# One piece of a maxima spread ahead of a bank copy in ScalarE's program

## The reference

```python
xn = layernorm(layernorm(x)) * ln_gamma + ln_beta
q, k, v = split(xn @ w_qkv)                   # 16 heads of 64; q and k are rotated (rope)
scores = einsum('bhid,bhjd->bhij', rotate(q), rotate(k)) * 64 ** -0.5
probs = softmax(scores)                       # over the 1024 keys j
x = x + (einsum('bhij,bhjd->bhid', probs, v) @ w_out + b_out)
x = x + fp4_linear(silu(gate) * up, w_down)   # gate, up = fp4_linear(layernorm(x), w_gate / w_up)
```

## Time and profile before

| what | before |
|---|---|
| median of 3 runs | 1604.24 us (1603.17 to 1604.52) |
| profiled execution | 1607.2 us, span of its instructions 1605.4 us |
| PE busy | 1512.1 us, 94% of the span |
| POOL busy | 1353.0 us, 84% |
| DVE busy | 1166.2 us, 73% |
| ACT busy | 890.3 us, 55% |
| max_rows pieces (L655) | 256 of 375 ns mean, 64 spreads |
| max_copy (L666) | 186 of 597 ns mean |

### The profile page before, as it was taken

The page is one execution under the profiler, slowest core; times in us unless marked ns, Lnnn a source line. Parts: engine busy times, 40 slices in busy tenths (PEclk is TensorE's granted clock), DMA queues, the critical chain, the costliest instruction groups (busy, mean ns, idle before and its releaser), DMA issues.

```text
span 1605.4 us, 25645 instructions
## 1 busy us (share of the span) xinstructions
PE 1512.1 (94%) x9257; PEld 789.6 (49%) x9257; DVE 1166.2 (73%) x1562; ACT 890.3 (55%) x1383; POOL 1353.0 (84%) x793
## 2 busy tenths in 40 slices
PE   3799999999999999999999999999999999998677
PEld 1345555445545554545545554555545455554455
DVE  4777777677777777776777777777777777763787
ACT  1265565655555665656555666655655665663222
POOL 4589999788889889898888988998888899976774
PEclk9699999999999999999999999999999999999798
DMA  4111111111111111111111111111111111100001
GB/s 131 45 28 47 48 43 44 47 47 43 28 47 47 34 47 47 40 48 47 42 35 40 48 34 47 48 39 47 47 44 45 29 47 36 41 17 23 7 14 33
DMA packets 69197, 67.10 MB, mean 42 GB/s; under 512 B 26512, under 2 KB 52432, under 8 KB 69072
## 3 DMA queue, kind: packets, MB, share of 16 engines
q1 hardware_dynamic: 69072, 65.46, 16.2%
HBM read 29.25 MB, written 2.62 MB: 20 GB/s over the span
## 4 chain that ended last, share of the span: by engine, by line
PE 82%; DVE 8%; ACT 5%; issue 4%; POOL 0%; DMA 0%; ACTq 0%; DVEq 0%
PE po L1130 29%; PE st L1117 18%; PE mx L1172 9%; PE ms L1153 8%; PE ms L1141 4%; PE ms L1198 4%; ACT max_rows L655 4%; PE ms L1189 4%; PE mx L1257 1%; PE ms L1180 1%; PE st L1257 1%; DVE negmax L871 1%; DVE probs L826 1%; DVE st L820 1%; DVE probs L1022 0%
## 5 line engine op out<-in xcount | busy, mean ns | idle before, releaser
L385 POOL TENSOR_TENSOR psum_keys<-psum_keys,probs 128x1024 f32<-128x1024 f32 x256 | 609.5, 2381 | 109.9 <-ACT probs L640 90.9
L640 ACT ACTIVATE probs<-st 128x1024 f32<-128x1024 f32 x512 | 498.5, 1030 | 131.0 <-PE st L1117 126.5
L1130 PE MATMUL po<-probs,v 128*64 128x512 f32 x2048 | 495.9, 605 | 0.0
L871 DVE TENSOR_REDUCE negmax<-mx 128x2 f32<-128x1024 f32 x318 | 388.3, 1221 | 125.8 <-PE mx L1172 125.6
L873 DVE TENSOR_REDUCE negmax<-mx 128x1 f32<-128x512 f32 x186 | 128.6, 691 | 215.8 <-PE mx L1172 215.8
L1130 PEld LDWEIGHTS po<-probs,v 128*64 128x64 f32 x2048 | 124.2, 136 | 256.2 <-issue 158.4
L1172 PE MATMUL mx<-keys_hi,queries_hi 64*128 64x512 f32 x1008 | 227.9, 448 | 9.2 <-ACT max_copy L666 5.4
L666 ACT ACTIVATE max_copy<-mx 128x512 f32<-128x512 f32 x186 | 111.1, 597 | 171.5 <-PE mx L1172 166.9
L1117 PE MATMUL st<-queries_hi,keys_lo 64*128 64x512 f32 x1024 | 204.0, 394 | 0.0
L1117 PE MATMUL st<-queries_lo,keys_hi 64*128 64x512 f32 x1024 | 202.1, 390 | 0.0
L1117 PE MATMUL st<-queries_hi,keys_hi 64*128 64x512 f32 x1024 | 201.8, 390 | 0.0
(11 more groups left out here) (161 smaller groups left out, 1803.5 us busy)
## 6 DMA issues: line engine op xcount, KB each, us to landing
kq<-sin_part SPq DMA_DIRECT2D x256, 128.0 KB, 2.4
rsum<-recips SPq DMA_DIRECT2D x128, 128.0 KB, 2.9
wqkv<-in_L_attn_w_qkv_dram SPq DMA_DIRECT2D x32, 192.0 KB, 2.8
resid<-in_L_attn_x_dram SPq DMA_DIRECT2D x4, 512.0 KB, 8.1
wout<-in_L_attn_w_out_dram SPq DMA_DIRECT2D x32, 64.0 KB, 2.6
out_dram<-resid SPq DMA_DIRECT2D x8, 256.0 KB, 2.3
sums<-sums_kept SPq DMA_DIRECT2D x64, 4.0 KB
spread<-sums SPq DMA_DIRECT2D x64, 4.0 KB, 1.6
```

What stands on the lines that cost most here:

```text
L385: nc.gpsimd.tensor_tensor(psum_keys[:, c], first, probs[:, (STEPS * P + i) % RING], ALU.add)\
L640: nc.scalar.activation(probs[:, step_n % RING], st[step_n % 2][:, :], ACT.Exp, scale=SCALE)\
L871: nc.vector.tensor_reduce(out, banks[:, :], AX.X, ALU.max, negate=True).then_inc(mx_free, 1)
L1130: last = mm(po[HD * a:HD * a + HD, :], v[:, P % 2, KEY_ORDER[jt], HD * a:HD * a + HD], probs[:, step_n % RING, a], start=(jt == 0), stop=( ...
```

## The change

In `spread_maxima` the call of `copy_ahead(P, d + 1)` moves from ahead of the spread to behind its first piece. The waits of the spread (for the transposition, for earlier scores, for the mask) are with that ahead of the copy, and the copy with its own waits is ahead of the other three pieces. No instruction is added or removed.

```diff
-        def spread_maxima(N, c):
+        def spread_maxima(N, c, P, d):
             filled(act, ("B", N, c))
             if N > 0 or c > 0:
                 act.wait_ge(st_ps, STEPS * (N - 1) + (JT if c == 0 else STEPS) + 2)
             act.wait_ge(mask_done, 1)
             for t in range(HALF):
                 last = nc.scalar.activation(max_rows[:, bass.ts(t, PART)], ms[:, 0:PART], ACT.Copy, scale=mask[:, t:t + 1])
+                if t == 0:
+                    copy_ahead(P, d + 1)
             last.then_inc(ms_free, 1)
...
                     if kind == "B":
-                        copy_ahead(P, d + 1)
-                        spread_maxima(X, u)
+                        spread_maxima(X, u, P, d)
```

## The result

The changed kernel takes 1590.84 us (median of 6 runs, 1590.47 to 1591.81), the kernel before 1604.59 in the same comparison (6 runs, 1603.17 to 1605.53): 13.75 us less, a ratio of 0.9914 with a 95% interval of 0.9903 to 0.9924. The forecast was 14.4 us less, and 1589.8 us. The profiled execution after has a span of 1588.7 us (1605.4 before) and a time of 1590.47 us. Three executions far out of line, two of the kernel before (1893.51 and 3633.75 us) and one of a variant (8068.79 us), are left out of all ratios.

The account below looks back on a forecast made before the run. TensorE bounds the kernel, held up by ScalarE's spread at 60 projections; 7.5 + 6.9 = 14.4 us won, other costs taken as 0, so 1604.24 us becomes 1589.8 us, range 1587 to 1598.

Parts of the forecast that it names:

- The ceiling of 0.25 and 0.23 us at 60 places: Projections behind a spread: at most 0.25 us at 30 places (L1153), 0.23 at 30 (L1198), 14.4 us in all.
- The 4% of max_rows in the chain: ScalarE's max_rows in the chain of waits: some 64 us of the span, said not to be what can be won.
- The piece lies in ScalarE's idle time and the copy is not late: ScalarE between transposition and copy: idle 2.64 us, copy has 0.25 us in hand; cost taken as 0.
- The rival that would have ended slower: ScalarE's queue: piece waits for the product, copy follows 0.39 us later; 8.4 us slower, 1612.6 us; chance 0.05.
- The release just meets TensorE's own earliest start: Bank ms free at 834.33, projection at 834.38, its undisturbed start; nothing to spare for L1153, 0.02 us for L1198.
- VectorE is next, and costs nothing: VectorE at the L1153 projections can follow by only 0.07 us for sure; its late mx release taken as 0 us.
- The 6.0 us that were kept for a late load: Weight load held for VectorE's mx release: if the matmul were as late, 0.20 us x 30 would go back.
- max_rows was to be gone from TensorE's waits: Sign of being right: max_rows gone from TensorE's waits and from the chain.
- TensorE's busy time was to stay the same: Sign of being right: TensorE's busy time unchanged while the span gets 14 us shorter.
- The six copy stalls shift with the rest: Six TensorE waits for the copied bank, 5.4 us in all: taken to cost 0 us, at most 1.5 us.

Follow-up runs that it names:

- Two and three pieces ahead: Two or three of the spread's four pieces ahead of the copy instead of one: 1590.41 us (ratio to before 0.9892) and 1590.88 us (0.9914).
- the extra piece behind: The change plus a useless fifth piece, written to an idle buffer, behind the copy: 1607.28 us, ratio to before 0.9999.
- d = 2 alone: One piece ahead of the copy only at d = 2, with d = 6 as in the kernel before: 1596.84 us, ratio to before 0.9951.
- the useless piece ahead: The change plus a useless fifth piece, written to an idle buffer, ahead of the copy: 1591.51 us, ratio to before 0.9901.
- the run with one memset: The change plus one tiny useless VectorE memset ahead of the rounding constants of y at three places: 1590.6 us, ratio to before 0.991.
- the four-ahead kernel: All four pieces of the spread ahead of the copy instead of one: 1607.02 us, ratio to before 1.0.

## Why the prediction was right, point by point

*The ceiling of 0.25 and 0.23 us at 60 places.* Right: the traces give 7.49 and 6.80 us for the 7.5 and 6.9. Two and three pieces ahead show that it is a ceiling, the extra piece behind that the release is what moves it, d = 2 alone that each place counts for itself. The 4% of max_rows in the chain were no measure of it, as the prediction said: the line has left the chain, and 0.9% of the time went.

*The piece lies in ScalarE's idle time and the copy is not late.* Right: the copy starts 0.85 us behind the transposition's start, 0.86 before. The rival that would have ended slower had its premise, that the copy keeps its place behind the piece on ScalarE, and lacked its occasion: the piece starts 0.36 us after the transposition's start and does not wait for the product.

*The release just meets TensorE's own earliest start.* Right: the projection starts 0.07 us after the last piece, where 0.05 was TensorE's reaction, and 0.32 us after the product, where 0.31 to 0.32 was its own earliest start. How little is to spare shows with the useless piece ahead: its last piece ends 0.03 us later than the change's, and the projections come 0.01 to 0.02 us later.

*VectorE is next, and costs nothing.* Right for the projections. In the changed kernel VectorE's release of mx comes at 829.34 + 1.17 = 830.51; the weight load is held to 830.57, some 0.06 us, and the product starts at 830.74, still 0.24 us behind the scores ahead of it. The 6.0 us that were kept for a late load did not come.

```profile
829.34 1.17 DVE L872 TENSOR_REDUCE negmax<-mx 128x2 f32<-128x1024 f32 x1
...
830.50 0.40 PE L1118 MATMUL st<-max_rows,one_rows 64*128 64x512 f32 x2
830.57 0.19 PEld L1173 LDWEIGHTS mx<-keys_hi,queries_hi 64*128 64x128 f32 x2
830.74 0.40 PE L1173 MATMUL mx<-keys_hi,queries_hi 64*128 64x512 f32 x2
```

*What it missed.* VectorE's three stalls, some 1.4 us in the traces (1.1 at the products, 0.3 behind them), were no term of the sum. With the spread released earlier VectorE comes to its constants ahead of a GpSimd addition's end and not behind the next one's start. That was luck, and could as well have gone the other way.

*Two signs that came otherwise.* max_rows was to be gone from TensorE's waits. It is gone from the matmuls' list; in the weight loads' list it stays, at the undisturbed 0.36 us. TensorE's busy time was to stay the same, and fell from 1512.1 to 1506.3 us. Some 4 us of that are no work saved, by an estimate from the rows: a projection 0.32 us behind a product that is 0.39 us long overlaps it by 0.07 us, at 60 places, and the overlap counts once. Most of the rest is the score matmuls' 1.9 us.

*The six copy stalls shift with the rest.* Right: 5.4 us before and after. Taken away, they are worth 7 us.

## What to carry to other kernels

The worth of a release is the smaller of two distances: how much earlier it can come, and how long the waiting engine could have started already. Read the second from a place where the same instruction pair runs undisturbed, not from the share of the chain. Where an in-order engine idles ahead of an instruction that waits, fill the idle time with work whose input is ready, until the waiting instruction becomes late; and look for the mirror case, where ready work stands ahead of an instruction that somebody waits for.

## What the runs showed of the hardware that was not expected

*A VectorE instruction 6 times as long, by when it starts.* The rounding constants, from SBUF to SBUF, take 0.37 to 0.43 us where nothing of GpSimd's holds them up. Begun behind an addition of GpSimd that still runs, they take what is left of it and 0.28 us, and never less than 0.37. In the kernel before:

```profile
635.25 2.38 DVE L839 TENSOR_SCALAR y_exp<-y_exp 128x512 f32<-128x512 f32 x1
...
634.97 2.37 POOL L385 TENSOR_TENSOR psum_keys<-psum_keys,probs 128x1024 f32<-128x1024 f32 x1
```

The addition ends at 637.34, the constants at 637.63. In the changed kernel they begin 0.07 us ahead of an addition's end, at 629.24, and take 0.38 us; in the run with one memset they come first, and GpSimd's addition is the longer one, by 0.22 us. In the thirteen traces the constants began 76 times while an instruction of GpSimd's ran. 70 times they began 0.07 us or more behind its start: where 0.08 us or more of it was left (53 times) they ended 0.28 to 0.29 us after it, where less was left they took 0.37 to 0.38 us. Six times they began 0.05 us or less behind it, took 0.37 to 0.38 us, and the addition was the longer one (2.61 to 2.66 us): so close together, the start times do not tell which of the two goes first. The Trainium skill has the rule (SBUF — State Buffer, Who interferes with whom): VectorE's second port pair is GpSimd's only one, an instruction such as tensor_scalar can take it in a two-port mode, and the one that issues first holds it for its whole length while the other waits. The runs agree in who waits and for how long, but for those six, and have 0.28 us on top; that the port is the cause, no run here separates from another.

*A matmul that starts after a wait holds up its successor too.* A maxima product that began on a release had its projection 0.43 us behind it, an undisturbed one 0.31 to 0.32. The 0.11 us are the mean of the 60 places in the four-ahead kernel, and the same at the six copy stalls.
